# More node rows fetched one by one by SyncE in a graph network's two attention passes: 16 and 12 chunks of units 117 and 118 in place of 9 of unit 123

## The reference

```python
def _gat(x, src, dst, W, att_src, att_dst, bias, n):      # twice
    xw = (x @ W).reshape(n, H, D)
    logits = leaky_relu(a_src[src] + a_dst[dst], 0.2)
    m = segment_max(logits, dst)
    ex = exp(logits - m[dst])
    alpha = ex / (segment_sum(ex, dst)[dst] + EPS)
    return segment_sum(xw[src] * alpha[..., None], dst).mean(axis=1) + bias
...
x = layernorm(x + L0(x, edges))                            # two _gat, with h @ lW + lb beside each
x = layernorm(x + L1(x, src, dst))                         # an attention of 128 channels over edges
```

## Time and profile before

| what | value |
|---|---|
| median of 3 runs | 5917.31 us (5913.04 to 5919.56) |
| the profiled execution | 5923.14 us, its span 5921.3 us |
| PE busy / DVE / ACT / POOL | 3916.7 us (66%) / 3698.7 (62%) / 2971.8 (50%) / 4430.4 (75%) |
| granted TensorE clock, mean | 0.605 |
| DMA moved | 447.03 MB, mean 75 GB/s |

### The profile page before, as it was taken

The page is one execution under the profiler, slowest core; times in us unless marked ns, Lnnn a source line. Parts: engine busy times, 40 slices in busy tenths (PEclk is TensorE's granted clock), DMA queues, the critical chain, the costliest instruction groups (busy, mean ns, idle before and its releaser), DMA issues.

```text
span 5921.3 us, 94392 instructions
## 1 busy us (share of the span) xinstructions
PE 3916.7 (66%) x22163; PEld 3603.6 (61%) x22163; DVE 3698.7 (62%) x9532; ACT 2971.8 (50%) x5708; POOL 4430.4 (75%) x4683
## 2 busy tenths in 40 slices
PE   5755555555556666666666666667777777777776
PEld 5655555555555555555555555567777777777776
DVE  5544444444445655555555555568888888888888
ACT  3433333333334355555555555556666666666665
POOL 7777777777777777777777777767777777777775
PEclk7656666655666656665555556666555555555556
DMA  7322222222223232322322222333333333333332
GB/s 168 81 63 63 64 64 63 63 63 63 60 62 69 59 68 67 66 67 67 67 67 67 67 66 65 66 77 91 89 90 89 86 90 90 90 89 90 90 90 67
DMA packets 334163, 447.03 MB, mean 75 GB/s; under 512 B 143370, under 2 KB 235602, under 8 KB 333372
## 3 DMA queue, kind: packets, MB, share of 16 engines
q0 software_dynamic: 149536, 217.14, 18.2%
q10 hardware_dynamic: 25824, 132.87, 7.1%
q1 hardware_dynamic: 158588, 94.96, 6.2%
HBM read 408.54 MB, written 40.09 MB: 76 GB/s over the span
## 4 chain that ended last, share of the span: by engine, by line
POOL 70%; issue 24%; PE 2%; DVE 2%; ACT 1%; POOLq 1%; DMA 1%; SPq 0%; DVEq 0%; ACTq 0%
POOL rows L1193 70%; PE psum L2318 1%; SPq L966 0%; DMA tab<-x_tab 0%; DVE mix L1529 0%; PE psum L2330 0%; ACT away L1889 0%; ACT L1932 0%; DMA w_heads<-in_L_gnn_W 0%; POOLq L1177 0%; ACT L1936 0%; PE psum L2260 0%; POOLq L1185 0%; DVE psum L1444 0%; DMA tab<-row_end 0%
## 5 line engine op out<-in xcount | busy, mean ns | idle before, releaser
L1193 POOL DMA_INDIRECT rows<-tab,idx_now x4623 | 4375.5, 946 | 1439.2 <-issue 1407.7
L2318 PE MATMUL psum<-share,rows 128*65 128x76 f32 (+10 forms) x6204 | 1164.5, 379 | 0.4 <-DVE share L1509 0.4
L1444 DVE TENSOR_TENSOR_SCAN psum<-cut,psum 48x224 f32<-48x224 bf16 (+3 forms) x524 | 450.4, 882 | 1076.8 <-PE psum L2290 1060.5
L2318 PEld LDWEIGHTS psum<-share,rows 128*65 128x65 f32 x6204 | 1080.7, 222 | 5.8 <-DVE share L1509 0.5
L2290 PE MATMUL psum<-ident,strip 128*48 128x128 f32 (+1 forms) x786 | 207.1, 400 | 1012.3 <-ACT strip L1923 1012.0
L2445 PE MATMUL psum<-own,hot_t 112*128 112x64 f32 x3126 | 646.5, 399 | 314.3 <-DVE mix L1716 311.8
L2445 PEld LDWEIGHTS psum<-own,hot_t 112*128 112x128 f32 x3126 | 624.9, 308 | 339.0 <-issue 242.8
L2290 PEld LDWEIGHTS psum<-ident,strip 128*48 128x48 f32 (+1 forms) x786 | 83.0, 132 | 1095.4 <-issue 1082.2
L2461 PE MATMUL psum<-hot,prob 128*128 128x112 f32 x3120 | 666.0, 408 | 5.0 <-DVE prob L1710 5.0
L2461 PEld LDWEIGHTS psum<-hot,prob 128*128 128x128 f32 x3120 | 647.2, 319 | 5.2 <-DVE prob L1710 5.2
L1891 ACT ACTIVATE hot_t<-away,ones 112x1536 bf16<-112x1536 f32 (+2 forms) x393 | 616.2, 1568 | 12.8
(11 more groups left out here) (284 smaller groups left out, 5627.6 us busy)
## 6 DMA issues: line engine op xcount, KB each, us to landing
rel_t<-rel_row ACTq DMA_DIRECT2D x128, 672.0 KB
rows<-tab,idx_now POOLq DMA_INDIRECT x4623, 2.5
rel_t<-rel_runs ACTq DMA_DIRECT2D x64, 672.0 KB
side_room<-tab SPq DMA_DIRECT2D x2304, 0.3 KB
own<-tab SPq DMA_DIRECT2D x262, 63.0 KB
cut<-cut_row SPq DMA_DIRECT2D x130, 120.2 KB
tab<-row SPq DMA_DIRECT2D x130, 112.0 KB
tab<-row SPq DMA_DIRECT2D x130, 63.0 KB
```

Of the source, the lines that this page charges most:

```text
L1193: nc.gpsimd.indirect_dma_start(rows_of[p][:, G * c.s + j, 0:D] if raw else rows_of[p][:, G * c.s + j, :], None, x if raw else halves[p], b ...
L1444: done = nc.vector.tensor_tensor_scan(running, cuts[:, 0:-1], values, NEG, ALU.add, ALU.max)
L2318: done = nc.tensor.matmul(summed[:, :, LO[j]:HI[j]], chunk_rows(c, j)[:, 0:D + 1], of[:, j, :, 0:SUBS[j]], start=not opened, stop=j == chu ...
```

## The change

It sets aside 16 chunks in pass 0 (all 12 of unit 117 and 4 of unit 118) and 12 in pass 1 (unit 117), and none of unit 123. POOL issues nothing for them. SP fetches 16 · 128 = 2,048 rows in pass 0 and 1,536 in pass 1, in 4 loops of 4 turns over 6 units each, that is units 6 to 101. A turn has 128 rows in pass 0 (21 or 22 in a unit) and 96 in pass 1 (16 in a unit). Where a unit has more than 16 rows, its source nodes come in two load instructions (10 or 11 values each); in pass 1 in one of 16. The sources of pass 1 are fetched into their tile anew in unit 4 of pass 1. The loops of all engines end at unit 113 instead of 119, in all three passes, and units 114 to 130 are written out. A path for a third pass is written, with 0 chunks.

```diff
-    SIDE, SIDES, SIDE_W = NU - 8, 9, 71
-    SIDE_LOOPS = 2
-    SIDE_TURNS = (NU - RING) // RING // SIDE_LOOPS - (1 if SIDE_LOOPS == 2 else 0)
-    SIDE_STEP = SIDES * P // (SIDE_LOOPS * SIDE_TURNS)
+    SIDE = NU - 14
+    SIDES, SIDE_W = (16, 12, 0), (71, 71, 131)
+    SIDE_LOOPS, SIDE_TURNS = (4, 4, 1), (4, 4, 0)
+    LOOPED = (NU - RING) // RING - 2
...
         def units(eng, end=NU):
-            with eng.Fori(1, (NU - RING) // RING) as q:
+            with eng.Fori(1, 1 + LOOPED) as q:
...
             def fetch_side_rows(p, c, h):
-                t0, t1 = [SIDE_STEP * (c.s + i) // RING for i in range(2)]
-                at = SIDE_STEP * (c.q - 1 - SIDE_TURNS * h)
-                _, nodes = nc.values_load_multi_w_load_instructions(side_src[h:h + 1, bass.ds(at + t0, t1 - t0)],
-                                                                    engines=(mybir.EngineType.SP,))
-                for t, node in zip(range(t0, t1), nodes):
+                block, each = P // SIDE_LOOPS[p], SIDES[p] // SIDE_TURNS[p]
+                turn = c.q - 1 - SIDE_TURNS[p] * h
+                t0, t1 = [each * block * (c.s + i) // RING for i in range(2)]
+                at = each * block * turn
+                half = (t0 + t1) // 2
+                for t2, t3 in ((t0, half), (half, t1)) if t1 - t0 > 16 else ((t0, t1),):
+                    _, nodes = nc.values_load_multi_w_load_instructions(side_home[p][h:h + 1, bass.ds(at + t2, t3 - t2)],
+                                                                        engines=(mybir.EngineType.SP,))
+                    for t, node in zip(range(t2, t3), nodes):
...
-                    if p < 2 and beside(c) == G:
+                    if p < 2 and beside(p, c) == G:
                         pool.wait_ge(sums_ready, n - RING + 2)
                         pool.sem_inc(go, 1)
-                    for j in range(beside(c) if p < 2 else 0, chunks(c)):
+                    for j in range(beside(p, c), chunks(c)):
```

More of the change, by code:

```diff
@@ L131, in came_aside @@
     def came_aside(p, c, count):
-        return sum(count(min(SIDES - G * i, G)) for before in range(2) for i in range(-(-SIDES // G))
+        return sum(count(min(SIDES[before] - G * i, G), 2 if before == 2 else 1)
+                   for before in range(3) for i in range(-(-SIDES[before] // G))
                    if (SIDE + i) % RING == c.s and (before < p or before == p and c.at_least(SIDE + i)))
     def first_landed(p, c):
-        return landed(p, c, 1, 1, 2, 2) - 16 * came_aside(p, c, lambda m: 1)
+        return landed(p, c, 1, 1, 2, 2) - 16 * came_aside(p, c, lambda m, first: first)
     def rest_landed(p, c):
-        return landed(p, c, G - 1, LASTC - 1, G - 2, LASTC - 2) - 16 * came_aside(p, c, lambda m: m - 1)
+        return landed(p, c, G - 1, LASTC - 1, G - 2, LASTC - 2) - 16 * came_aside(p, c, lambda m, first: m - first)
     def chunks(c):
@@ L613, in units @@
                 yield Unit(u // RING, u % RING)
[L614 removed]
+            with eng.Fori(1, 1 + LOOPED) as q:
                 for s in range(RING):
                     yield Unit(q, s)
[L617 removed]
+            for u in range(RING * (1 + LOOPED), end):
                 yield Unit(u // RING, u % RING)
@@ L1082, in units_aside, with fetch_side_sources @@
-            def units_aside():
+            def fetch_side_sources(p):
+                block, n = P // SIDE_LOOPS[p], SIDES[p]
+                to = side_home[p].rearrange("h (k e) -> h k e", e=block)
+                if p < 2:
+                    edges = src[UE * SIDE:UE * SIDE + n * P].rearrange("(k h e) -> h k e", h=SIDE_LOOPS[p], e=block)
+                    sp.dma_start(to, edges).then_inc(dst_aside_in, 16)
+                else:
+                    for h in range(SIDE_LOOPS[p]):
+                        for i in range(block // QUAD):
+                            edges = bass.AP(src.tensor, UE * SIDE + RUN * (block // QUAD * h + i), [[1, 1], [QUAD, n], [1, QUAD]])
+                            sp.dma_start(to[h:h + 1, :, QUAD * i:QUAD * i + QUAD], edges).then_inc(dst_aside_in, 16)
@@ new lines, in fetch_side_rows @@
+            def fetch_side_rows(p, c, h):
+                block, each = P // SIDE_LOOPS[p], SIDES[p] // SIDE_TURNS[p]
[7 more added lines that the diff above has]
+                    for t, node in zip(range(t2, t3), nodes):
+                        r = block * h + t % block
+                        row = side_rows[p][r:r + 1, bass.ds(each * turn + t // block, 1), 0:SIDE_W[p]].rearrange("p a w -> p (a w)")
+                        at_w = HALF if p < 2 else 4 * D - SIDE_W[p]
+                        sp.dma_start(row, tab[p][bass.ds(node, 1), at_w:at_w + SIDE_W[p]]).then_inc(side_in[p], 16)
@@ L1111, in _ @@
                 fetch_cuts(p, unit(2))
-                for c, h in units_aside() if p < 2 else ((c, None) for c in units(sp)):
+                for c, h in units_aside(p) if SIDES[p] else ((c, None) for c in units(sp)):
                     n = NU * p + c.u
@@ L1131, in _ @@
                         sp.dma_start(src_wide, src[0:UE].partition_broadcast(W)).then_inc(end_in, 16)
[L1132 to L1140, removed]
+                    if p == 0 and SIDES[0] and c.below(5) and c.at_least(4):
+                        fetch_side_sources(0)
+                    if p > 0 and SIDE_LOADS[p] and c.below(5) and c.at_least(4):
+                        fetch_side_sources(p)
+                    if SIDE_LOADS[p] and c.below(RING) and c.at_least(RING - 1):
+                        sp.wait_ge(dst_aside_in, 96 + 16 * sum(SIDE_LOADS[0:p + 1]))
                     if not c.below(1):
```

117 lines of the change are left out of this document (66 added, 51 removed).

## The result

The changed kernel takes **6197.93 us** (median of 4 runs, 6190.92 to 6202.0) against 5915.61 us of the kernel before in the same comparison (4 runs): ratio 1.0475 [1.0458, 1.0491]. The prediction said 6134 us, 6070 to 6260. Its profiled execution took 6195.58 us with a span of 6193.7 us (before 5923.14 and 5921.3), at a mean granted clock of 0.612 (before 0.605).

What follows compares the result with a forecast made beforehand. POOL bounds the kernel before; after the change SP sets pass 0's pace at 17.98 us a unit. 5923.1 + 234 − 17.6 = 6139.5 us, given as 6134 since the profiled execution is 5.8 above the median; range 6070 to 6260.

Steps and rivals of the forecast that it cites:

- What bounds the kernel: Kernel before: POOL issues without a stop, 1.251 us a transfer, 15.0 us a unit; a chunk taken away is worth 1.25 us.
- SP's unit in pass 0: Pass 0: SP's work per unit rises from 10.88 us by 4.91 for rows and 2.19 for loads to 17.98, against POOL's 15.0.
- odd tens: Pass 0: two of a turn's four loads of 10 values begin at odd places; 1.11 to 2.23 us each, 1.67 taken.
- Price of the loads: SP's source-node loads: 10 values 1.11 us from even places, 11 values 2.45 us from even or odd places.
- The turn's end: SP's loop turns in pass 0: every new loop pays the branch's fetch stall, 2.6 / 6 = 0.43 us a unit.
- The gate: Pass 0: SP's delay reaches POOL through the stored row and ACT's front; unit s + 9 ends some 12 us after row s's store.
- The sum for unit 110: Pass 0: store of row 101 at 1903.4 us, POOL's unit 110 ends at 1915.4 instead of 1681.7, +234 us; break-even 15.55 us a unit.
- What it gives: Savings: pass 0 −8.8 us, pass 1 −3.8, shorter waits before pass 2 −5; together −17.6 us.
- Pass 1: SP's work per unit in pass 1 rises from 12.40 to 14.4 us, below 15.0, so nothing on the path.
- The rival with 3.56 us: Pass 1 is SP-bound too: the 16-value load costs 3.56 us, SP works 16.4 us a unit, kernel 6196 us; chance 0.2.
- the halves are cheap: Pass 0: both loads of a unit cost 2.4 us together, SP takes 16.2 us a unit, kernel 5960 us; chance 0.07.
- SP has the room: Pass 0: SP stays under 15.55 us a unit, rows at most 0.34 us each, delay never reaches POOL; 5900 us; chance 0.05.

Runs made afterwards that it cites:

- the aligned kernel: The changed kernel (16 and 12 chunks), but every load of sources in pass 0 begins at a multiple of 4 values, same rows: 5935.43 us (one run).

## Why the prediction was right

**What bounds the kernel.** Right. POOL's 1.25 us a chunk holds in both kernels, and POOL alone at work from unit 111 on: from 1982.6 to 2251.0 us for units 111 to 130.

**SP's unit in pass 0.** Right in kind, 0.55 us short. The 81 units from 455 to 1955 us, set against the 44 of the earlier trace rows, show where. The loads of a unit took 4.38 us for 4.19, since both odd tens took 2.23. The added rows, each with the gap ahead of it, took 5.10 us for 4.91: a row costs 0.475 us in both kernels, and 0.46 was only the difference of two groups. The address instruction ahead of the second load, which I had left out, takes 0.14. The turn's ends cost 0.09 less than I had kept: 12 of the 16 take 2.90 to 3.30 us, but the last turn of each of the four loops, behind which no branch goes back, takes 0.59 to 0.96. The remaining 0.1 us or so lies in the rest of the unit and was not traced. The working gave an upper bound of 18.60; 18.53 lies just in it, but by other terms: of its two, the tens at 2.23 came true and the stall twice as long did not.

**Price of the loads.** The two groups of the trace were read by the wrong property. I took length (10 or 11) and evenness of the place as candidates. What the runs show is whether the load starts at a multiple of 4: from there, 8, 12 and 16 values take 0.69, 0.91 and 1.14 us, thus 0.24 us and some 0.056 us a value. Values left over behind the last whole group of four, and all values of a load that starts elsewhere, cost about 0.2 us each (10 values: 1.11 from a multiple of 4, 2.23 from elsewhere; 11 from elsewhere 2.43, 12 from elsewhere 2.63). In the kernel before all loads of 10 happened to start at a multiple of 4 and none of the loads of 11 did, so that its trace could not tell length from place. The Trainium skill's page "Runtime: NRT & Kernel Launch", section "Instruction fetch mechanics", has about 200 ns a register even in bulk: the loads off a multiple of 4 agree with it (2.43 / 11 = 0.22), those of whole groups don't, and the measurement decides. The page speaks there of registers loaded from device memory, while these loads read a tile.

**The turn's end.** The same section of the Trainium skill's page has a taken branch whose target is outside the window of two pages wait for the fetch of its page, and gives no size. The trace agrees in that the 2.9 us or more stand only where a branch goes back. But not each such branch pays: in the second loop of the kernel before, with the same body, 0.70 to 0.77 us lie behind the last row of a turn. Which pages lie in the window no run here shows. A turn of the new loops of pass 0 has 521 instructions in the trace, not "well over" 512.

**The gate.** Here a step failed. I had SP's delay reach POOL through the stored row and the front that ACT makes, with POOL's unit s + 9 ending 12 us after the store of row s. It goes through the cut marks: 1.4 us ahead of the store of row s, SP fetches those of unit s + 4, DVE waits for them, and behind its scan stand the sums of unit s + 3, which release the last chunk of POOL's unit s + 8. The run with the rows ahead of the store shows it: the store came 15 us later against the cut marks, and POOL stayed with the cut marks. In the steady state POOL's unit s + 8 ends 8 to 9 us after the store of row s (867.05 and 875.6; 1958.6 and 1967.6), and unit 110 then takes POOL's own 15.0 us: 24 us behind the store of row 101, not 12. ACT's wait at `row_front` for the stored row, which I had named as a sign, does not appear among its waits.

**The sum for unit 110.** Forecast +233.7 us. Measured +300.9: 2.6 for a later store of row 5, 52.6 for 0.55 us in 96 units, 12.0 for the release. These make the 67.2 us more. The break-even is then (1681.7 − 24 − 179.9) / 96 = 15.4 us a unit, not 15.55, and e.g. the aligned kernel at 15.83 is just above it.

**What it gives.** Forecast −17.6 us behind unit 110, measured 300.9 − 272.4 = −28.5. Pass 0 gave 9.3 (forecast 8.8), pass 1 8.1 (3.8; the rest is a slow drift of POOL's spacing, 944 for 946 ns busy), the waits before pass 2 fell from 18.9 to 11.8 us, 7.1 (forecast 5), and pass 2 drifted by another 3.6.

**Pass 1.** Right: SP waits 88.5 us in the 92 units from 2420 to 3800 us, 0.96 us a unit (forecast 0.6), and works 14.0 (forecast 14.4), since 16 values cost 1.14 us, less than either of my two values. The rival with 3.56 us is refuted by that row.

**The other rivals.** That the halves are cheap is refuted as the change stands, but the aligned kernel is that rival made true: 5935 us, even below the 5960 that I gave for it. That SP has the room is refuted: a row costs no less when 21 stand together, 0.475 us, where the rival wanted at most 0.34.

So the miss of 64 us is 67 us at unit 110, less 11 us gained behind it, and the rest is the difference between the profiled execution and the medians. The range held, but with some luck: the bounds of the forecast alone ended at 6194 us, 4 us below what was measured. The part above them was there for the rival of pass 1, which is refuted; what filled it was the gate's 12 us.

## What to carry to other kernels

An engine without a busy share in the page can be the next bound: take its waits off the period of the loop, and what is left is its work. Add up every instruction that a moved transfer costs, its address work and its register load too, against the period, before the transfers' bytes; beyond the break-even each further unit of work is paid in full, times the number of units. Before a queue takes more, look for the cheap saving in it: here the start of a load of registers was worth 2.7 us a unit, 262 us in all.

## What the runs showed of the hardware

- A load of several registers from a tile is cheap only in whole groups of 4 values, and only if it starts at a multiple of 4: 12 values in 0.91 us from such a place, and in 2.63 from another.
- One SP transfer of 71 numbers with dynamic source costs 0.46 to 0.48 us of SP's time, address work and gaps included, and 21 in a row cost no less each.
- The branch back at a turn's end can hold SP up: 2.90 to 3.30 us lie between the last row and the next cut marks at 12 turns of the changed kernel's pass 0, 0.59 to 0.96 where the loop ends. In one loop of the kernel before, the same branch costs 0.70 to 0.77 us.
- Two chips of those used ran the kernel before in 7746 and 7773 us instead of 5916, with gaps of 0.70 us ahead of some of SP's instructions, POOL's transfers being as short as elsewhere (0.95 us). There even 12 chunks lose 5%.
- Loads whose values are not used are not in the program that runs; a count in the trace shows it.
